# Local attention: each tile's output projection behind the next tile's turn, the residual with it

## The reference, cut to what matters

```
h = shift_token(x);  q, k, v = split(h @ wqkv, 3)          # 8 heads of 64
q = l2norm(q) * qs;  k = l2norm(k) * ksc;  q, k = rotary_xpos(q, k)
o = local_attention(q, k, v)          # windows of 64, each sees itself and the one before
x = x + o @ wo                        # the output projection and the residual
h = shift_token(x);  h = (h - mu) / sqrt(var + 1e-5) * lg + lb
a, g = split(h @ w1 + b1, 2);  x = x + (a * gelu(g)) @ w2 + b2
```

## Time and profile before

| | us |
|---|---|
| median of 3 runs | 724.11 |
| the runs | 724.12, 723.22, 724.11 |
| profiled execution, its own time | 724.43 |
| its span (first to last instruction) | 722.6 |

### The profile page before, as it was taken

How to read it: one execution, slowest core, us unless ns; L and a number is a source line. 1 busy time by engine, 2 the same in 40 slices (tenths; PEclk the granted TensorE clock), 3 DMA queues, 4 the chain that set the end, 5 groups by cost and what they waited for, 6 DMA issues and landing times.

```text
span 722.6 us, 16005 instructions
## 1 busy us (share of the span) xinstructions
PE 626.0 (87%) x5547; PEld 433.4 (60%) x5547; DVE 567.9 (79%) x1451; ACT 489.3 (68%) x1423; POOL 386.1 (53%) x425
## 2 busy tenths in 40 slices
PE   2799997888999979998999997997899999997533
PEld 1366654555666666564666666665677777776312
DVE  5667778797999976869999997655677777777586
ACT  1578775687888883559888888343677777865333
POOL 5848767898999931668999993111012121112300
PEclk9999999999999999999999999999799999999775
DMA  7700000110111110012111110000000000000002
GB/s 227 172 2 1 1 5 9 23 24 16 24 24 28 26 60 16 6 22 53 24 23 24 24 31 16 1 2 0 1 1 2 1 2 1 2 2 1 0 0 59
DMA packets 20219, 17.28 MB, mean 24 GB/s; under 512 B 7234, under 2 KB 15884, under 8 KB 20044
## 3 DMA queue, kind: packets, MB, share of 16 engines
q1 hardware_dynamic: 19308, 16.25, 9.1%
q10 hardware_dynamic: 832, 0.00, 0.1%
HBM read 8.91 MB, written 1.05 MB: 14 GB/s over the span
## 4 chain that ended last, share of the span: by engine, by line
PE 43%; POOL 32%; DVE 10%; ACT 7%; issue 7%; DMA 0%; POOLq 0%; SPq 0%; DVEq 0%; ACTq 0%
POOL rsk L500 7%; POOL rsq L500 6%; POOL rot L617 5%; POOL rot L604 5%; PE PS L994 4%; POOL rot L610 4%; PE PS L1019 3%; POOL btmp L495 3%; PE PS L882 3%; PE PS L900 3%; PE PS L901 3%; PE PS L975 3%; PE PS L1004 3%; ACT pc L1296 2%; PE PS L967 2%
## 5 line engine op out<-in xcount | busy, mean ns | idle before, releaser
L1223 ACT ACTIVATE pc<-PS,nb,rsq 128x128 f32<-128x128 f32 x256 | 113.9, 462 | 1.0 <-DVE nb L1605 0.3
L808 PE MATMUL PS<-wqkv,hB 128*128 128x512 f32 x192 | 104.2, 626 | 3.9 <-DVE rsin L1591 1.6
L1296 ACT ACTIVATE pc<-PS,nb 128x256 f32<-128x256 f32 x128 | 59.0, 473 | 46.7 <-DVE nb L1787 46.7
L500 POOL TENSOR_TENSOR rsk<-btmp,neghalf 128x8 f32<-128x8 f32 x32 | 59.9, 1873 | 5.9 <-POOL btmp L495 5.9
L817 PEld LDWEIGHTS PS<-ident,rot 128*128 128x128 f32 x256 | 31.7, 143 | 47.9 <-issue 28.5
L1787 DVE TENSOR_REDUCE nb<-PS 128x2 f32<-128x512 f32 x64 | 40.8, 679 | 24.1 <-PE PS L994 24.1
L500 POOL TENSOR_TENSOR rsq<-btmp,neghalf 128x8 f32<-128x8 f32 x32 | 54.0, 1688 | 5.9 <-POOL btmp L495 5.9
L1614 DVE TENSOR_TENSOR pc<-pc,rden 128x512 f32<-128x512 f32 x64 | 53.4, 835 | 2.2
L1223 ACT ACTIVATION_READ_ACCUMULATOR pc<-PS,nb,rsq 128x1 f32 x256 | 53.2, 208 | 0.0
L1587 DVE TENSOR_TENSOR rot<-PS,xeff 128x512 f32<-128x512 f32 x64 | 44.1, 689 | 10.2 <-ACT sq L1211 9.6
L1601 DVE TENSOR_REDUCE mx<-PS 128x4 f32<-128x512 f32 x64 | 43.6, 681 | 8.5 <-PE PS L835 8.5
(11 more groups left out here) (236 smaller groups left out, 1719.8 us busy)
## 6 DMA issues: line engine op xcount, KB each, us to landing
V<-V SPq DMA_DIRECT2D x48, 128.0 KB, 2.2
wqkv<-in_L_ffn_wqkv SPq DMA_DIRECT2D x2, 768.0 KB, 5.4
out<-x SPq DMA_DIRECT2D x4, 256.0 KB, 2.3
x<-in_x SPq DMA_DIRECT2D x1, 768.0 KB, 6.8
ctxT<-in_ctxT SPq DMA_DIRECT2D x1, 768.0 KB, 6.8
w<-in_L_ffn_w SPq DMA_DIRECT2D x2, 341.0 KB
ctxs<-in_ctx SPq DMA_DIRECT2D x1, 576.0 KB, 8.6
gel<-in_bands SPq DMA_DIRECT2D x1, 512.0 KB, 8.9
```

The costliest lines, as they stand in the source:

```text
L500: return tt(dst, tmp, neghalf[:, 0, 0:tmp.shape[1]], ALU.pow)
L808: i = mm(ps, hB[:, b % 2, j * P:(j + 1) * P], wqkv[:, w * INNER:(w + 1) * INNER], start=True, stop=True)
L1223: i = af(pc[:, g % 2, par, c * P:(c + 1) * P], c_bank(g, par)[:, c * P:(c + 1) * P], ACT.Exp, bias=nb[:, g % 2, at], scale=rsq[:, g % 8, 2 ...
L1296: i = af(pc[:, u % 2, par, n * S:(n + 1) * S], c_bank(u, par)[:, n * S:(n + 1) * S], ACT.Exp, bias=nb[:, u % 2, par * 2 + n:par * 2 + n + ...
```

## The change

Two places. The list of pieces has W first in `B_MID` instead of last in `B_END`, so that PE issues it directly behind the turn; and DVE's `b_residual` is called behind `b_scale(g + 1, 1)` instead of behind `b_turned(1, ...)`.

```
-B_MID = ["t", "k", "kT"]
-B_END = ["v", "qT", "q", "W"]
+B_MID = ["W", "t", "k", "kT"]
+B_END = ["v", "qT", "q"]
...
                 if 0 <= step + 1 < T:
                     b_scale(g + 1, 1)
+                if step >= 1:
+                    b_residual(layer, step - 1)
                 if step == T - 4:
                     f_shifted(layer * 4)
                 if 0 <= step + B_AHEAD["k"] < T:
                     b_turned(0, g + B_AHEAD["k"])
...
                 if step >= T - 2:
                     f_gate(layer * 4, step - T + 2)
-                if step >= 1:
-                    b_residual(layer, step - 1)
                 if step == T - 4:
                     f_apply(layer * 4)
```

## The result

The changed kernel takes 740.85 us (median of 4 runs, 739.99 to 741.61) against 723.95 for the kernel before (4 runs, 723.22 to 724.12): 16.9 us more, ratio 1.0229 with a 95% interval of 1.02 to 1.0259. The forecast was 745.0 and the range 735 to 753.

What follows compares the result with a forecast made beforehand. The prediction took a loop through the residual and kT's PSUM bank to set the 8.57 us step, POOL a close second. 22.4 + 1.3 + 1.0 - 4.0 = +20.7 us gave 745 us, range 735 to 753.

Steps and rivals of the forecast that it cites:

- sign that it named for "right": Trace marks expected: period 9.9 us, kT's load waiting on the residual, L1614 held by POOL's L617, DVE idle.
- (a): On PE, W moves behind the turn; its new wait for DVE's copy is nothing, so steady steps lose nothing.
- (b): On DVE, the residual behind L1614 starts 1.32 us later, and the steady period grows from 8.57 to 9.89 us.
- the loop through the residual: Residual, kT, q, ACT's square, DVE's rotation, next residual: claimed to set the 8.57 us period, air at most 0.1.
- (c): Steady steps of both layers: 17 loops lose 1.32 us each, +22.4 us in all (low end 13.8).
- (d): First steps of the layers' local attention: +1.3 us in layer 1, +1.0 in layer 0 (0 to 2.1).
- (e): Steps 13 to 16 of each layer: W fills PE's waits, -2.0 us per layer, -4.0 in all.
- Rival 1: Steady steps: L1614 gets ahead of POOL's L617, so only 0.81 us lost a step; 735 us, chance 0.12.
- Rival 2: Steady steps: the wait only changes place, if kT has 1.3 us to spare; 724 us, chance 0.04.
- Rival 3: Faster: steady steps absorb the delay, W gains 2.2 us at each layer's end; 719.7 us, chance 0.07.
- Rival 4: PE's new gaps lower its clock in 17 steps, 1.5 us each, 26 us on top; 771 us, chance 0.04.

Runs made afterwards that it cites:

- first experiment: The changed kernel with DVE's residual put directly ahead of L1611 and L1614 of par 1, W still behind the turn: 720.59 us, ratio 0.9932 to the kernel before.
- second experiment: The kernel before with PE's order kept and only DVE's residual moved behind L1611 and L1614 of par 1: 748.71 us, ratio 1.0332.

## Why the prediction was right, and which terms were off

**The mechanism and the sign (right).** The residual behind L1614 delays kT of the same step, PE's load waits for it up to 1.8 us, DVE stands idle ahead of L1587 and L1601, and POOL waits for rsin. Each sign that it named for "right" is in the trace, but for the size of the period.

**(a) W behind the turn costs nothing (right).** The first experiment has W there and a step of 8.57, though W starts 1.02 behind the turn instead of 0.87, held by the copy to `oT` (the wait taken as nothing was 0.15); in the changed kernel a W of a quarter its size leaves the step at 9.66.

**(b) +1.32 per loop (right in the delay, wrong in what of it arrives).** The residual is late by 1.30. But "no link in it has more than 0.1 us of air" was the step that failed. kT followed the residual by 0.51, and needs only 0.33, so the loop through the residual had 0.18 of air; 0.05 more came back between kT and q (4.53 instead of 4.58), where the bands no longer wait for ACT's copies. 1.30 - 0.18 - 0.05 = 1.07, measured 1.09. I had taken kT's start as set by the residual and compared it with "k's start plus 0.86"; it was 0.97 whatever the residual did, as qT follows v by 0.96 (205.79 to 206.75). The statement that the loop through the residual sets the period was wrong: **it is 0.2 us shorter than the 8.57**, which by the rows is the length of ACT's loop, and the loop through k's bank lies between the two. The runs give this air three times over, and a delay smaller than it costs nothing:

| | residual behind q's rot | delay | step | step less 8.57 |
|---|---|---|---|---|
| before, first experiment | 1.80 | 0 | 8.57 | 0 |
| between L1611 and L1614 | 1.88 | 0.08 | 8.57 | 0 |
| changed, without L617 | 2.62 | 0.82 | 9.19 | 0.62 |
| changed | 3.10 | 1.30 | 9.66 | 1.09 |
| behind k's rotation | 5.01 | 3.21 | 11.57 | 3.00 |

The last column is the delay less 0.2, and 0 where the delay is smaller.

**(c) 17 loops (count nearly right).** The two stretches of steady steps, 19 of them, grew by 8.56 and 11.02, together 19.6; the forecast for them, with layer 1's start, was 8 x 1.32 and 9 x 1.32 + 1.3 = 23.7. At 1.09 it would have been 8.7 and 11.1. The whole error is the 0.23 per loop.

**(d) The starts (right in layer 1, open in layer 0).** Layer 1's 11.02 less 9 x 1.09 leaves 1.2 against the forecast 1.3. In layer 0 1.05 against 1.0, but 0.84 of that has nothing to do with the change, so its true size may be anything from 0.2 up to 1.

**(e) -2.0 at each end (right once).** Layer 0 gave 1.90. Layer 1 gave 0.67, because PE's clock fell there after a gap of the same length as in layer 0:

```profile
269.93 1.09 PE L845 MATMUL PS<-ident,pc 128*128 128x128 f32 x8 [1.50 <-DVE pc L1614]
271.42 1.13 PE L813 MATMUL PS<-woB,oT 128*128 128x128 f32 x8 [0.40 <-DVE oT L1619]
...
460.20 1.09 PE L845 MATMUL PS<-ident,pc 128*128 128x128 f32 x8 [1.51 <-DVE pc L1614]
461.69 1.83 PE L813 MATMUL PS<-woB,oT 128*128 128x128 f32 x8 [0.40 <-DVE oT L1619]
```

Between 461.69 and 465.16 the granted clock was 0.53. The two experiments that keep the gain of the ends have 1.6 to 1.9 per layer, and the two kernels without L617 differ there by 2.1 in each layer, so 2.0 was about right where the clock stayed up.

**The rivals.** Rival 1 (L1614 runs at once) is excluded by the 1.18 us of L1614; the run without L617 shows the step that it would have had, 9.19. Rival 2 had the right question, how much air kT has: 0.2 us, not 1.3 and not 0.1. Rival 3's gain exists, 3.3 to 3.7 us, and is had without the loss by the first experiment. Rival 4 did not come in the steady steps, though the run with the short W shows it nearer than "the new gaps are about 1.4" made it: another 0.81 us of idle time in the step brings it in five of eighteen.

**The sum.** Forecast +20.7; with 1.09 in place of 1.32 in 17 loops it would have been +16.8, against 16.9 in the medians. In the profiled pair the same with -0.67 at the second end and -2.25 of other work gives the 15.8. That the medians meet the corrected sum to 0.1 is luck, since each of these two terms is larger than that.

Five correct orders are faster than both kernels, by 0.3 to 0.8%: with W behind the turn, the residual ahead of L1611 (720.59), between L1611 and L1614 (719.64) or ahead of q's sums (718.46), or the first of these with k ahead of t (721.12); and W moved in the last steps alone (722.21). Between the first four the measurement can't tell.

## What to carry to other kernels

When an operation that frees a buffer is moved back in an engine's queue, look for the loop that runs through it, and for the other loops that have the same length within tenths: what arrives in the period is the delay less the difference to the longest, here 1.30 less 0.2. The longest need not run through the busiest engine: by the rows it is ACT's here, which has 7.66 us of work in 8.57. To find the air, ask of each instruction in the loop how soon it could follow its releaser (kT 0.33 behind the residual, not 0.51), and look for short waits in the rows of the weight loads and in the distances between starts, since the matmul's own row may show none. A run that makes one engine's work shorter brings such a wait out, but it does not show that the wait sets the period: k waited 0.81 us in one run, and taking that wait away left the step at 8.57. And a move of work into an engine's idle time and a move of its consumer are two changes: done apart, the first gained 4 us and the second lost 24.

## What was not expected of the hardware

- A 128x512 fp32 multiplication on DVE (L1614) takes 0.70 us alone and 1.18 beside POOL's 1.27 us addition. It ends 0.54 to 0.56 behind POOL's end however early it starts: 0.17 us ahead of that end (residual ahead of q's sums), 0.44 (the kernel before) or 0.64 (the changed kernel).
- PE's granted clock after gaps is not a matter of one gap's length: after 2.8 to 2.9 us it fell in 14 of 20 steps, after 1.5 us in one of two, with 0.97 alone in a steady step in none, but with 0.97 and 0.81 in the same step in five of eighteen, and in the second experiment in one step with 0.76 and 0.97, though not in one with 1.20 and 1.18. A fall cost 1.2 us at the end of layer 1 and 1.5 to 1.6 in most steps.
- Less work on PE made the changed kernel 2 us slower by this (742.97 against 740.85), and at the ends of the kernel before with the short W too: 8.42 us at a granted clock of 0.59, where the same stretch took 6.99 at 1.00 with the full W.
